# A graph network on one core: nine buffers of gathered rows in place of six, and eight slots of dense blocks in place of seven

## The reference: what is computed

```python
# first layer: ten steps over the same weighted graph
wn = w * inv_sqrt_out[s] * inv_sqrt_in[d]          # edges and self loops
def step(h, _):
    agg = segment_sum(h[s] * wn[:, None], d, num_segments=n)
    return ((1.0 - ALPHA) * agg + ALPHA * feat_0, None)
h, _ = scan(step, feat, None, length=10)
x = layernorm(x + h)
# second layer: attention over the edges, once
score = Kh[src] * Qh[dst] / sqrt(8) * Eh           # 8 heads of 8
score = exp(clip(score.sum(-1), -5, 5))
out = layernorm(x + segment_sum(Vh[src] * score, dst))
```

## Time and profile before

| | us |
|---|---|
| median of 3 runs | 12354.14 |
| profiled execution | 12366.96 |
| its span | 12365.2 |
| PE matmul busy | 9373.4 (76%) |
| POOL busy | 7320.9 (59%) |
| DVE busy | 6074.0 (49%) |
| ACT busy | 4835.6 (39%) |

### The profile page before, as it was taken

How to read it: one execution, slowest core, us unless ns; L and a number is a source line. 1 busy time by engine, 2 the same in 40 slices (tenths; PEclk the granted TensorE clock), 3 DMA queues, 4 the chain that set the end, 5 groups by cost and what they waited for, 6 DMA issues and landing times.

```text
span 12365.2 us, 147377 instructions
## 1 busy us (share of the span) xinstructions
PE 9373.4 (76%) x50360; PEld 5442.0 (44%) x50360; DVE 6074.0 (49%) x15582; ACT 4835.6 (39%) x6399; POOL 7320.9 (59%) x7701
## 2 busy tenths in 40 slices
PE   5974776998989889798998989989898544454455
PEld 5974774333334334333333334333333544444444
DVE  8763664454444544444444444544445344444445
ACT  1321222554555545454554555545455100101111
POOL 5666655665656566565665656666565355555554
PEclk5555555998989989898998989989899566666666
DMA  9951223886878878787887878868786444433333
GB/s 313 408 217 30 57 53 113 294 293 244 293 247 294 280 257 296 245 298 244 294 298 241 298 248 293 299 241 297 246 290 243 115 108 109 108 106 107 107 105 97
DMA packets 1386471, 2696.97 MB, mean 218 GB/s; under 512 B 684032, under 2 KB 714659, under 8 KB 1385718
## 3 DMA queue, kind: packets, MB, share of 16 engines
q1 hardware_dynamic: 958006, 2245.72, 50.7%
q0 software_dynamic: 248000, 261.74, 9.2%
q10 hardware_dynamic: 179712, 180.00, 4.7%
HBM read 2454.23 MB, written 232.42 MB: 217 GB/s over the span
## 4 chain that ended last, share of the span: by engine, by line
PE 53%; another core or an unknown queue 14%; DVE 14%; issue 13%; POOL 3%; DMA 2%; ACT 1%; DVEq 0%; SPq 0%; ACTq 0%; POOLq 0%
PE banks L2297 38%; PE banks L2348 5%; PE banks L2266 4%; POOL arena L1632 3%; DVE arena L1895 2%; PE banks L2267 2%; DVE arena L2174 2%; PE banks L2341 1%; DVE arena L2173 1%; DVE arena L1928 1%; DVE arena L2182 1%; DVE arena L2181 1%; DVE arena L2233 1%; DVE arena L2180 1%
## 5 line engine op out<-in xcount | busy, mean ns | idle before, releaser
L1632 POOL DMA_INDIRECT arena<-node_rows,src_idx x4800 | 4580.8, 954 | 2871.8 <-issue 1276.7
L1701 ACT ACTIVATE arena<-arena 128x1024 f32<-128x1024 f32 x4084 | 4037.2, 1047 | 3377.7 <-DMA arena<-dense 1391.6
L2297 PE MATMUL banks<-arena 128*64 128x512 f32 x12240 | 2916.7, 615 | 151.1 <-issue 111.2
L2297 PE MATMUL banks<-arena,u_sb 128*64 128x512 f32 x11760 | 2800.0, 615 | 182.5 <-issue 108.3
L1646 POOL DMA_INDIRECT arena<-kv_rows,src_idx x1568 | 1497.1, 955 | 1269.1 <-DVEq L2234 686.2
L2297 PEld LDWEIGHTS banks<-arena 128*64 128x64 f32 x12240 | 1050.3, 142 | 1701.0 <-issue 1616.5
L2071 DVE SCALAR_TENSOR_TENSOR arena<-arena,banks 128x1024 f32<-128x1024 f32 x816 | 993.1, 1218 | 1568.8 <-DMA arena<-dense 668.5
L2297 PEld LDWEIGHTS banks<-arena,u_sb 128*64 128x64 f32 x11760 | 996.1, 142 | 1688.7 <-issue 1576.6
L2040 DVE TENSOR_SCALAR arena<-banks,rel,w_tab 128x128 f32<-128x128 f32 x4800 | 1604.4, 405 | 120.8 <-issue 10.5
L2266 PE MATMUL banks<-arena 128*128 128x98 f32 x3136 | 1141.8, 468 | 597.9 <-ACT arena L1680 537.6
L1603 POOL DMA_INDIRECT dense<-arena x1012 | 1054.5, 1042 | 673.6 <-issue 284.5
(11 more groups left out here) (244 smaller groups left out, 5381.8 us busy)
## 6 DMA issues: line engine op xcount, KB each, us to landing
arena<-dense SPq DMA_DIRECT2D x3550, 512.0 KB
dense<-blank SPq DMA_DIRECT2D x5, 26112.0 KB
arena<-in_dst_dram SPq DMA_DIRECT2D x195, 512.0 KB
arena<-node_rows,src_idx POOLq DMA_INDIRECT x4800
arena<-in_edge_attr_dram SPq DMA_DIRECT2D x195, 256.0 KB
u_sb<-key_rows ACTq DMA_DIRECT2D x26, 1792.0 KB
dense<-blank SPq DMA_DIRECT2D x1, 44800.0 KB
arena<-key_rows ACTq DMA_DIRECT2D x23, 1792.0 KB
```

Of the source, the lines that this page charges most:

```text
L1632: gp.indirect_dma_start(out=rows_in[:, n % ROWS, s, :], out_offset=None, in_=node_rows[k % 2], in_offset=bass.IndirectOffsetOnAxis(ap=src_ ...
L1701: nc.scalar.activation(planes[:, q % PLANES, half, :], ring[:, n % SLOTS, :], ACT.Relu, scale=-1.0 if half else 1.0).then_inc(planes_act, 1)
L2297: done = mm(banks[h * D:(h + 1) * D, sum_slot(k, g), :], u, rows[:, h * 512:(h + 1) * 512], start=first, stop=last, tile_position=(0, h * ...
```

## The change

`ROWS` goes from 6 to 9 and `SLOTS` from 7 to 8, and the arena grows by 2560 elements in each partition (3 x 384 for the rows, 1024 for the slot, and some spare), in SBUF that was free. Each new buffer and slot has a semaphore of its own. No instruction is added, removed or moved on any engine. What changes is which buffer an instruction names, and which earlier event it waits for: the gathers of an iteration wait for the scatter nine iterations back in place of six, and a load for the item eight loads back in place of seven.

```diff
-SLOTS = 7
+SLOTS = 8
 PLANES = 4
-ROWS = 6
+ROWS = 9
...
-ARENA = 29696
+ARENA = 32256
```

## The result

| | before | after |
|---|---|---|
| median of four runs, us | 12360.67 | 12602.19 |
| lowest and highest | 12351.62, 12385.58 | 12579.16, 12626.22 |
| profiled execution | 12366.96 | 12602.76 |
| its span | 12365.2 | 12601.0 |

The change makes the kernel 1.9% slower: the ratio is 1.0186, 95% interval [1.0168, 1.0203]. 12602 lies in the range of the prediction (12465 to 12640); the kernel lost 241.5 us where +203 was forecast. (One execution of all that follow, 14065.46 us at a clock of 0.567 in `r3s7_slow`, was slow and is in no comparison.)

The account below looks back on a forecast made before the run. PE sets the pace mid-step; at a step's start it slows beside POOL's unbroken gathers. 208 + 32 - 27 - 10 = +203 us gives 12570 by the profiled execution, forecast as 12557 us, 1.6% slower; range 12465 to 12640 us.

Parts of the forecast that it names:

- The longer row: Step's start: 62 unbroken gathers instead of 44 lengthen PE's slow stretch by 22.7 us, costing 20.8 us a step, +208 us.
- Once more round: Step boundaries: iteration 1's scatter in time frees a buffer, adding six gathers without pause; half of nine boundaries, +32 us.
- PE's crawl: Beside long unbroken gather rows, PE starts single matmuls with idle time marked "issue", 0.47 a microsecond, a twelfth of full pace.
- Nine buffers in the middle: Middle of a step: three fewer iterations have gathers beside them, 0.9 us each, -27 us in ten steps.
- The eighth slot: Dense-block loads: one more block lands ahead, cutting PE's waits for planes; gain between 0 and 101 us, taken as 10.
- second round: Step boundaries: six more gathers prolong the row when iteration 1's scatter is in time; +32 us, bounds 0 and +63.
- The crawl that ends by itself: Rival, step boundary: PE's slow stretch keeps its old length whatever the gather row; 12344 us, chance 0.07.
- The double runs: Rival, middle of a step: POOL's rows of twelve gathers vanish; five of nine gone gives 12207 us, chance 0.06.
- The Trainium skill's rule: Contention comes only from the port pair shared by VectorE and GpSimd; PE never waits on anyone, so gathers cannot slow it.

Follow-up runs that it names:

- r3s7_slow: Slow execution named for three buffers of gathered rows and seven slots, against six buffers in the kernel before; 14065.46 us at a clock of 0.567.
- mix1: Kernel before with nine buffers, seven slots, and a different gather lead or pauses in each step; 12326.88 us against 12365.97, one execution each.
- r9s7: Nine buffers in place of six, seven slots kept, against the kernel before; 10149.15 us against 10150.81, ratio 0.9999.

## Why the prediction was right, and where it was not

*The longer row: right.* Forecast 62 gathers, a row 22.7 us longer and 20.8 us a step. The row has 62 in all ten steps, and in steps two to ten iteration 2 is scattered 22.5 us later. The term was 1.7 us too small. PE does start more matmuls from the first gather to the end of the row, 92 where it was 84 as a mean of these steps, but it comes back later: the first six starts within 2 us begin 8.6 us behind the last gather's end, before 5.7. The two cancel. In the first step the row grew from 38 gathers, not 44, and iteration 2 is scattered 32.5 us later.

*Once more round: wrong.* It was counted at +32 us and happened in none of the nine boundaries. The step that failed is that a scatter in time frees its buffer in time. At the boundary shown, the last matmul of iteration 1's scatter started at 2895.54, 11.9 us before the last gather ended. But VectorE's addition of that window, which waits for the scatter, started at 2916.80, and POOL's next gather, which waits for it too, at 2917.04; the trace has the semaphore `scattered` step at 2916.78, some 21 us behind the matmul. In four of the nine boundaries the last matmul started before the row's end, in five 0.0 to 6.3 us behind it, and in all nine the semaphore stepped 9.4 to 9.5 us behind the last gather's end. PE's crawl holds up its signals too. So, in these boundaries, the row could not prolong itself.

*Nine buffers in the middle: not seen.* Forecast -2.7 us a step; from the scatter of iteration 2 to that of 77 a step of steps two to ten became 0.8 us longer, within the spread of the steps. In mix1 iterations 12 to 77 take 584 and 575 us at a lead of three, 587 at two, 576 at four, 578 and 580 at six, and 576 and 573 at nine. That may be a small gain of a long lead; with two steps at three that differ by 9 us it shows none.

*The eighth slot: no gain seen.* PE's waits for ACT went from 179.1 to 185.6 us and those for DVE from 23.1 to 21.9, so the forecast -10 is not to be seen, and 0 fits as well. Alone it ran on a chip without the crawl only (0.9996), where POOL hides it. That it isn't the cause of the loss mix1 shows, with seven slots.

*Sum.* The forecast was 208 + 32 - 27 - 10 = +203. What came, up to the scatter of iteration 2, is nine times 22.5 and 32.5 in the first step, +235.3; behind it nine times 0.8 and -13.6 in the first step, -6.6; and no second round. That is +228.7 of the 235.8 by which the profiled executions differ; the steps begin 1.7 us later, and 5 us lie in the attention layer. So the row was 27 us more than its term, the second round was 32 us that did not come, and the gains of 37 us came to 7. The mechanism was right; that the total came so near is in part luck, since these misses cancel.

*The rivals.* The crawl that ends by itself is refuted by mix1. The double runs did not go away: the second step has eight, where it had nine, and the ten steps have 82 before and 82 after (the prediction had taken nine in each, 90).

*The cause.* I had written that I take the row of gathers as the cause. On a chip with the crawl mix1 shows it: shortening, cutting or moving the row does the same to the crawl. But it is half of the cause. On the other chips the same row, 482 gathers long, leaves PE at 5.8 starts in a microsecond. What the chips with the crawl have that the others lack is open; gathers take 1.26 us on both. The prediction's 12557 was a number for one kind of chip, and its profile could not have told that. The Trainium skill's rule ("SBUF — State Buffer", section "Who interferes with whom"), which I had weighed as speaking against the mechanism, agrees with the chips without the crawl, where each half of the change costs nothing (0.9999 and 0.9996); the whole change was not timed on one. On the others the measurement decides: PE does wait, in whatever way. What it waits for remains open too, but one rival can be struck out. The transfers that run in the last 27 us of the row shown above and up to PE's return at 2915.84 are the gathers alone (window 2880 to 2916; an instruction transfer would have a line of its own):

```profile
q0 software_dynamic: 736, 0.76, 11.8%
```

At the starts of all ten steps after the change, no instruction transfer starts in the 38 us before PE returns, and the next one starts behind its return. Beside a stretch as early in the row of r9s7 (2447 to 2504) four run. So PE does not come back because one lands.

*Left open for want of such a chip:* three buffers, the eighth slot alone, and pauses at a short lead, for the whole program on a chip with the crawl. By mix1's steps three buffers take 732 us where six take about 750, and 722 where the kernel before's last step takes 743. That would be worth some 18 to 21 us a step. It is argued from two steps of one execution (3 and 10) and not shown as a time.

## What to carry to other kernels

More buffers ahead are not free when the producer can fill them in one unbroken row: ask what the rest of the chip does during that row, and read it in the matmul starts, not in the busy share. Depth beyond what the waits ask for (15 us of waits here) has little to gain. A pause in the producer helps only if it removes the row and costs less than the row did: ten pauses at a step's start merely moved it. And time a small change on more than one chip before believing either answer: here each half of the edit is worth 1.000 on one chip, and the whole of it 1.018 on another.

## What the runs showed of the hardware

- The same program took 12361 to 12371 us in some comparisons and 10143 to 10151 in others on other chips, 18% less, within 0.1% among themselves. The second step takes 751 us before and 619 in r9s7. Of these 132 us, 42 lie before the scatter of iteration 2 (at 71.8 and 29.9 us), beside the row, and 91 between it and that of iteration 77 (664.7 and 573.8 us). Nine double runs at the prediction's 7 us each would make some 63 of the 91, an estimate; the rest is not accounted for.
- In a crawl PE starts 0.42 matmuls in a microsecond against 5.8 on the chips without it, and signals from PE reach the engines that wait for them up to 21 us late; on r9s7's chip the same signal steps 0.3 to 0.4 us behind the start of the last matmul.
- 7.99 us an iteration, taken for PE's best, is not: without the crawl an iteration takes 7.6 us (2320 starts in 400 us, 44 to an iteration), the pace of POOL's six gathers.
- An indirect gather of 128 rows keeps POOL busy for 0.95 us and the next starts 1.26 us behind it, on both kinds of chip, with or without the crawl.
- A pause of 2 us behind every six gathers keeps the crawl away, and at a lead of nine costs as much as it gains (771 us a step against 769 and 772). Where there is no crawl, the same pause costs its own length.
